# First pass of a decoder layer: the state sums of two neighbouring units done together on TensorE

## The chip, the cores and the metric

The kernel runs on one core of one Trainium2 chip. The metric is device time in microseconds of one execution, lower is better. Times given for the kernel are the median of several runs; the rows shown come from one profiled execution.

## The reference, cut to what matters

The layer takes 128 sequences of 128 tokens with 256 features and passes them through a Mamba block, a cross-attention block with a state-space convolution, and a feed-forward block with nine paths. The change lies in the Mamba block (inner width 512, 16 states):

```python
xz = einsum('bld,ed->ble', x, in_proj_w);  xc, z = split(xz, 2)
xs = silu(causal_conv(xc, conv_w) + conv_b)
dt, Bm, Cm = split(xs @ x_proj_w.T, [64, 80])
dt = softplus(dt @ dt_proj_w.T + dt_proj_b);  A = -exp(A_log)
# over the tokens, for each channel d and state n:
h[d, n] = exp(dt[d] * A[d, n]) * h[d, n] + dt[d] * Bm[n] * xs[d]
y[d] = sum_n h[d, n] * Cm[n] + D[d] * xs[d]
out = (y * silu(z)) @ out_proj_w.T
```

Then, in the same pass of the kernel, the first half of cross attention: query and key projections, scores of 4 heads, the 32 largest of each row, softmax over them, their mean over heads times the context, and the linear maps (film) that scale and shift the normed input.

## The kernel before

Everything is float32. The kernel has a set-up part and three passes. The first pass does the Mamba block and the attention part, the second the state-space convolution, the third the feed-forward block. Only the first pass is touched.

The first pass works in 32 blocks of four sequences (512 columns). A block has 64 units, `u` = 0 to 63: four chunks `c` of 128 channels by 16 states `n`, so a unit is the scan of one state of one chunk over 512 columns. Each engine has its own program with a loop over the units; they meet through semaphores that count (`need(engine, name, i, k)` waits until event `name` of block `i` has happened `k` times). What a unit does:

- ScalarE writes the decay exp(dt A) (L1044), into PSUM for an even unit and into SBUF for an odd one.
- The input term dt B x is made in two ways. For an even unit GpSimd multiplies it into the ring (L1263, event `bx`). For an odd unit ScalarE scales it in transposed form (L1031, `bxt`), and TensorE transposes it back with four transposes (`spread_bx`, L860, `bxp`), one unit ahead (`PE_AHEAD` = 1).
- VectorE runs the scan (L1175 for odd units, L1179 for even ones, event `scan`) into a slot of a ring of eight (`RING` = 8).
- GpSimd multiplies the state by C (L1250, event `hc`), four units behind (`POOL_LAG` = 4).
- TensorE adds the product to y in PSUM, a matmul with the identity (`sum_states`, L875, event `nsum`), also four units behind (`SUM_LAG` = 4). The first sum of a chunk (`n` = 0) also starts the bank with diag(D) times xs (L874). This frees the slot of the ring: the input product or scan eight units on waits for it. After the 16th sum of a chunk ScalarE copies y out (L1022) at unit `n` = 2 of the next chunk.

Between these, each engine runs "steps" at fixed units, from tables `PE_AT`, `ACT_AT`, `DVE_AT` and `POOL_AT` (step name: unit). Steps of `FRONT` prepare the next block `i + 1`, steps of `BACK` finish block `i - 1`. On TensorE the even units with steps are 2, 6, 8, 10, 14, 22, 24, 26, 30, 34, 36, 40, 42, 44, 54, 56, 58, 60 and 62. The steps that the text speaks of:

- `sc0` to `sc3` (units 22, 29, 36, 45): scores of one sequence, one bf16 matmul for the mask (L817) and four heads with 32 rows each (L824). All four use one bank: `sc2` waits until VectorE has read the bank for sequence 1 (`em`, L1147), at the end of a search in four rounds (`tka` to `tkd`, L1132 and L1136) and the exponentials on ScalarE (`sm`, L989 and L993). `qk` (unit 21) makes q and k, copied out by ScalarE (k in L984).
- `xp` (unit 24): x_proj (L745), needs ScalarE's silu (L928); `bt` (unit 26): transposes of B and C (L758), need ScalarE's copy of x_proj (L936).
- `dt0` to `dt3` (L752), read by ScalarE (L950, L952); `ds0` to `ds3` (L774 and after), the softplus sum, copied by ScalarE (L966) and multiplied by GpSimd (L1242).
- `op0` to `op3` (L785): out_proj; `tu0` to `tu3` (L767): transposes of dt x, copied by ScalarE (L942); `xc0` to `xc3` and `z0` to `z3` (L739): in_proj, with the convolution's taps on VectorE (L1099).

All steps but the scores share two PSUM banks in turn, so a step also waits until the tile before the last has been read (`take_bank`). TensorE's program is in order: a step or sum that waits holds up what is behind it.

Of the kernel before, what the change touches and what calls it, by code (L numbers as in the profile page):

```python
# [49 lines left out]
SUM_LAG = 4  # L50
# [57 lines left out]
def steps_at(table, u, which):  # L108

    return [s for s, at in table.items() if at == u and s in which]  # L110
# [35 lines left out]
def through_pe(u):  # L146

    return u % 2 == 1
# [340 lines left out]
def pass1(nc, sems, i_, arena, psum, x1_d, xa_d, xin_d, wf_d, bc_d, kr_d, sh, NB):  # L489
    with ExitStack() as ctx:  # L490
# [77 lines left out]
        def need(eng, name, i, k):  # L568

            count = i * PER[name] + k  # L570
            if not isinstance(count, int) or count > 0:
                eng.wait_ge(S[name], count)
# [12 lines left out]
        def which_steps(front, back):  # L585
            return (FRONT if front else []) + (BACK if back else [])
# [125 lines left out]
        def _(pe):  # L712
# [140 lines left out]
            def spread_bx(i, u):  # L853

                v = u // 2
                need(pe, "bxt", i, v + 1)
                j, w = before(i, u, 4)
                need(pe, "scan", j, w + 1)
                for b in range(G):
                    mm = pe.transpose(bx_ps[:, v % 2, b * L:(b + 1) * L], bxt[:, v % 2, b * P:(b + 1) * P], ident)  # L860
                mm.then_inc(S["bxp"], 1)

            def sum_states(i, par, u):
                if u < 0:
                    i, par, u = i - 1, 1 - par, C * NS + u
                need(pe, "hc", i, u + 1)
                c, n = u // NS, u % NS
                if n == 0:
                    if c == 0:
                        need(pe, "y", i - 1, C)  # L870
                    else:
                        need(pe, "y", i, c)

                    pe.matmul(y_ps, diag_d[:, c], xs[par][:, c], start=True, stop=False)  # L874
                pe.matmul(y_ps, ident, ring[:, u % RING], start=False, stop=n == NS - 1).then_inc(S["nsum"], 1)  # L875

            def iteration(i, par, front, back):
                which = ([True] if front else []) + ([False] if back else [])
                names = which_steps(front, back)
                for u in range(C * NS):  # L880
                    w = u + PE_AHEAD
                    if through_pe(w):
                        if w < C * NS:
                            spread_bx(i, w)
                        elif front:
                            spread_bx(i + 1, w - C * NS)
                    if u >= SUM_LAG or back:
                        sum_states(i, par, u - SUM_LAG)
                    for s in steps_at(PE_AT, u, names):
                        if s in FRONT:  # L890
                            step(s, i + 1, 1 - par, i - 1, which)
                        else:
                            step(s, i - 1, 1 - par, i + 1, which)
# [7 lines left out]
            for u in range(PE_AHEAD):  # L901
                if through_pe(u):
                    spread_bx(0, u)
            all_blocks(pe, iteration, NB)
            for u in range(SUM_LAG):
                sum_states(NB, 0, u - SUM_LAG)
# [1029 lines left out]
```

## Time and profile before

| | |
|---|---|
| runs, us | 7264.4, 7266.84, 7272.13; median 7266.84 |
| profiled execution, us | 7281.31 |
| its span, us | 7279.5 |
| mean granted TensorE clock | 0.947 of full |
| first pass | from about 250 us to 5100 us of the span |
| busy share of the span | TensorE 92%, VectorE 74%, GpSimd 63%, ScalarE 61% |

Times in the profile are microseconds from the start of the span unless marked ns. A line of the timeline gives start, duration, engine, source line, operation, destination and source with their shapes, and how many instructions of one kind in a row were merged (x4). In brackets stand the idle time of the engine before it and what ended it. A float32 matmul over 512 columns is two records, each with a weight load on a row of its own (PEld). Matmuls overlap, so the sum of durations is more than the time that passes. DVE is VectorE, ACT ScalarE, POOL GpSimd. The whole of a block is some 152 us; the rows below are from one block in the middle (2500 to 2650 us) where not said otherwise.

### The profile page before, as it was taken

The numbers are of one execution on the slowest core, as the hardware profiler recorded it, in microseconds if no ns is written. First come the engines' busy times: TensorE is split into PE (matmuls) and PEld (weight loads), VectorE is DVE, ScalarE is ACT, GpSimd is POOL, SyncE is SP. The second block draws the span as 40 slices with busy tenths as digits, with TensorE's granted clock in tenths as the row PEclk, the third lists the DMA queues.
The fourth block names the chain that finished last, engine by engine and source line by source line (L and its number), as shares of the span: only waits on it lengthen the run. The fifth ranks groups of instructions, "written<-read, shape, count | busy, mean of one in ns | idle before, by whom it ended". The sixth has DMA issues, their size and how long they took to land. (4 is left out here: it accounts for less than half of the span.)

```text
span 7279.5 us, 106079 instructions
## 1 busy us (share of the span) xinstructions
PE 6712.2 (92%) x24272; PEld 3702.6 (51%) x24272; DVE 5405.5 (74%) x13962; ACT 4456.3 (61%) x9788; POOL 4589.0 (63%) x3991
## 2 busy tenths in 40 slices
PE   2899999999999999999999999997789999999997
PEld 1354444544445444454445544454656666666664
DVE  5588888888888888888888888887436666666665
ACT  2778888788877888878888788885212112221111
POOL 0788888888888888888888888897011112111111
PEclk6999999999999999999999999998889999999998
DMA  1666556665666666666556655566611111111110
GB/s 42 137 142 151 140 144 156 154 146 144 143 150 153 147 144 143 152 153 149 143 135 151 158 147 144 137 151 176 208 35 33 32 32 32 32 32 32 32 32 20
DMA packets 554199, 834.94 MB, mean 115 GB/s; under 512 B 169180, under 2 KB 207389, under 8 KB 551713
## 3 DMA queue, kind: packets, MB, share of 16 engines
q1 hardware_dynamic: 552768, 820.23, 46.1%
q10 hardware_dynamic: 864, 8.65, 0.3%
q8 instruction: 174, 2.85, 0.2%
q14 instruction: 393, 3.21, 0.1%
HBM read 745.91 MB, written 74.45 MB: 113 GB/s over the span
## 5 line engine op out<-in xcount | busy, mean ns | idle before, releaser
L1250 POOL TENSOR_TENSOR arena<-arena 128x512 f32<-128x512 f32 x2048 | 2581.9, 1276 | 276.4 <-DVE arena L1175 249.2
L875 PE MATMUL psum<-arena 128*128 128x512 f32 x4096 | 2192.3, 632 | 43.7 <-POOL arena L1250 37.9
L1175 DVE TENSOR_TENSOR_SCAN arena<-arena,psum 128x512 f32<-128x512 f32 x1024 | 1237.2, 1208 | 385.4 <-ACT arena L1044 297.9
L1263 POOL TENSOR_TENSOR arena<-arena 128x512 f32<-128x512 f32 x1024 | 1331.6, 1300 | 149.8 <-PE psum L875 149.5
L1031 ACT ACTIVATE arena<-arena 128x128 f32<-128x128 f32 x4096 | 1304.8, 396 | 134.0 <-PE psum L860 133.6
L1179 DVE TENSOR_TENSOR_SCAN arena<-psum,arena 128x512 f32<-128x512 f32 x1024 | 1234.8, 1206 | 87.4 <-ACT psum L1044 26.0
L875 PEld LDWEIGHTS psum<-arena 128*128 128x128 f32 x4096 | 712.0, 199 | 599.0 <-issue 385.4
L1044 ACT ACTIVATE arena<-arena 128x508 f32<-128x508 f32 x1024 | 738.5, 721 | 57.8 <-DVE arena L1175 57.1
L1829 POOL TENSOR_SCALAR arena<-arena 128x4 f32<-128x4 f32 x160 | 37.0, 231 | 1164.9 <-DVE arena L1690 1164.9
L860 PEld LDWEIGHTS psum<-arena 128*128 128x128 f32 x4096 | 518.7, 146 | 489.2 <-issue 441.4
L1044 ACT ACTIVATE psum<-arena 128x508 f32<-128x508 f32 x1024 | 701.5, 685 | 64.8 <-DVE arena L1179 31.0
L860 PE MATMUL psum<-arena 128*128 128x128 f32 x4096 | 648.1, 283 | 27.1 <-DVE arena L1175 12.5
L1653 ACT ACTIVATE arena<-psum,arena 128x512 f32<-128x512 f32 x256 | 176.5, 690 | 621.6 <-PE psum L1560 621.6
L739 PE MATMUL psum<-arena 128*128 128x512 f32 x1024 | 479.7, 597 | 29.9 <-ACT arena L1068 27.5
L1560 PE MATMUL psum<-arena 128*128 128x512 f32 x1024 | 449.9, 597 | 1.4 <-ACT arena L1647 1.4
L1571 PE MATMUL psum<-arena 128*128 128x256 f32 x2048 | 447.2, 379 | 0.0
L1571 PEld LDWEIGHTS psum<-arena 128*128 128x128 f32 x2048 | 388.9, 190 | 66.7 <-issue 15.4
L1136 DVE MATCH_REPLACE8 arena<-arena 128x128 f32<-128x128 f32 x1536 | 407.1, 278 | 0.0
L1838 POOL TENSOR_TENSOR arena<-arena 128x1024 f32<-128x1024 f32 x32 | 75.3, 2353 | 448.1 <-DVE arena L1728 448.1
L1099 DVE SCALAR_TENSOR_TENSOR arena<-psum,arena 128x508 f32<-128x508 f32 (+2 forms) x384 | 282.6, 743 | 98.7 <-ACT arena L919 89.5
L739 PEld LDWEIGHTS psum<-arena 128*128 128x128 f32 x1024 | 195.6, 192 | 277.7 <-issue 267.6
L1132 DVE MAX8 arena<-arena 128x8 f32<-128x128 f32 x1536 | 327.8, 277 | 7.7
(218 smaller groups left out, 10103.8 us busy)
## 6 DMA issues: line engine op xcount, KB each, us to landing
arena<-bc_scratch SPq DMA_DIRECT2D x1152, 512.0 KB, 5.3
arena<-in_xT_dram SPq DMA_DIRECT2D x32, 512.0 KB
arena<-in_x_dram SPq DMA_DIRECT2D x32, 512.0 KB, 7.8
x_scratch<-arena SPq DMA_DIRECT2D x32, 512.0 KB, 5.7
xin_scratch<-arena SPq DMA_DIRECT2D x128, 128.0 KB, 2.5
arena<-kernel_scratch SPq DMA_DIRECT2D x32, 512.0 KB, 7.0
arena<-x_scratch SPq DMA_DIRECT2D x32, 512.0 KB, 3.8
out_dram<-arena SPq DMA_DIRECT2D x32, 512.0 KB
```

Of the source, the lines that this page charges most:

```text
L739: mm = pe.matmul(ps, win[:, k, e0:e0 + P], xT[:, k], start=k == 0, stop=k == DH - 1)
L860: mm = pe.transpose(bx_ps[:, v % 2, b * L:(b + 1) * L], bxt[:, v % 2, b * P:(b + 1) * P], ident)
L875: pe.matmul(y_ps, ident, ring[:, u % RING], start=False, stop=n == NS - 1).then_inc(S["nsum"], 1)
L1031: a = act.activation(bxt[:, v % 2, b * P:(b + 1) * P], uT(par, c)[:, b * P:(b + 1) * P], ACT.Identity, scale=BT[par][:, b, state(u):state( ...
L1044: act.activation(seqs(decay)[:, :, 1:L], seqs(dt[par][:, c])[:, :, 1:L], ACT.Exp, scale=negA[:, c, k:k + 1]).then_inc(S["decay"], 1)
L1136: a = dve.match_replace(left[:, h], v8[:, r, h], src[:, h], NEG)
L1175: dve.tensor_tensor_scan(s, decay_sb[:, u // 2 % 2], bx_ps[:, u // 2 % 2], 0.0, ALU.mult, ALU.add)\
L1179: dve.tensor_tensor_scan(s, decay_ps[:, u // 2 % 2], s, 0.0, ALU.mult, ALU.add)\
L1250: pool.tensor_tensor(h, h, Cb[:, u // 2 % PAIRS, u % 2], ALU.mult).then_inc(S["hc"], 1)
L1263: pool.tensor_tensor(ring[:, u % RING], uu[par][:, c], Bb[:, state(u)], ALU.mult)\
L1560: mm = pe.matmul(psum[:, m % 2], w1[:, k, m * P:(m + 1) * P], hT[:, k], start=k == 0, stop=k == DH - 1)
L1571: mm = pe.matmul(psum[:, 2 + o, bb * D:(bb + 1) * D], gT[:, m, b * L:(b + 1) * L], w2[:, m], start=m == 0, stop=m == 7)
```

## The change

In TensorE's loop over the units the state sum that lies four units behind used to be issued in every unit, ahead of the unit's steps. Now an even unit issues none, and an odd unit issues two: the one that lies five units behind (the even one) and the one that lies four behind. The transposes of `spread_bx`, which are issued in even units, so stand between the pairs. Nothing else is edited.

```diff
                         elif front:
                             spread_bx(i + 1, w - C * NS)
-                    if u >= SUM_LAG or back:
-                        sum_states(i, par, u - SUM_LAG)
+                    if u % 2:
+                        for w in (u - SUM_LAG - 1, u - SUM_LAG):
+                            if w >= 0 or back:
+                                sum_states(i, par, w)
                     for s in steps_at(PE_AT, u, names):
                         if s in FRONT:
                             step(s, i + 1, 1 - par, i - 1, which)
```

## Rows read from the trace of the kernel before

**Rows 1.** The page, part 1: busy us, share of the span, instructions.

```profile
PE 6712.2 (92%) x24272; PEld 3702.6 (51%) x24272; DVE 5405.5 (74%) x13962; ACT 4456.3 (61%) x9788; POOL 4589.0 (63%) x3991
```

**Rows 2.** Groups by line and shape, 1000 to 5000 us: busy, mean, idle before, releaser.

```profile
L1250 POOL TENSOR_TENSOR arena<-arena 128x512 f32<-128x512 f32 x1685 | 2124.7, 1276 | 223.9 <-DVE arena L1175 206.1 <-DVE arena L1179 14.3 <-DMA arena<-bc_scratch 1.9
L875 PE MATMUL psum<-arena 128*128 128x512 f32 x3366 | 1800.9, 631 | 30.0 <-POOL arena L1250 25.9
...
L875 PEld LDWEIGHTS psum<-arena 128*128 128x128 f32 x3366 | 584.7, 199 | 481.1 <-issue 314.4 <-POOL arena L1250 157.6
```

**Rows 3.** Timeline of TensorE around scores 2: start, us, engine, line, count, idle before.

```profile
2552.58 1.88 PE L875 MATMUL psum<-arena 128*128 128x512 f32 x4
...
2558.69 1.10 PE L874 MATMUL psum<-arena 128*128 128x512 f32 x2
2559.62 1.02 PE L875 MATMUL psum<-arena 128*128 128x512 f32 x2
...
2565.02 0.60 PE L817 MATMUL psum<-arena 1*128 1x512 bf16 x1 [3.32 <-DVE arena L1147]
...
2568.52 2.08 PE L875 MATMUL psum<-arena 128*128 128x512 f32 x2
```

**Rows 4.** Timeline of VectorE from scores 0 to unit 31.

```profile
2533.83 0.89 DVE L1132 MAX8 arena<-psum 128x8 f32<-128x128 f32 x4 [0.70 <-PE psum L824]
...
2550.39 1.20 DVE L1175 TENSOR_TENSOR_SCAN arena<-arena,psum 128x512 f32<-128x512 f32 x1
```

**Rows 5.** Timeline of all engines, units 22 to 26.

```profile
2530.15 0.59 ACT L984 COPY arena<-psum 128x512 f32<-128x512 f32 x1 [1.08 <-PE psum L806]
...
2531.49 0.38 PE L817 MATMUL psum<-arena 1*128 1x512 bf16 x1
...
2533.83 1.91 ACT L928 ACTIVATE arena<-arena 128x2048 f32<-128x2048 f32 x1
...
2535.91 3.60 PE L745 MATMUL psum<-arena 128*96 128x512 f32 x8
...
2541.26 0.57 ACT L936 COPY arena<-psum 96x512 f32<-96x512 f32 x1
...
2541.92 0.40 PE L758 MATMUL psum<-arena 32*128 32x32 f32 x4 [0.26 <-issue]
```

**Rows 6.** Timeline of TensorE at unit 30, the transposes for unit 31.

```profile
2548.68 0.66 PE L860 MATMUL psum<-arena 128*128 128x128 f32 x4
```

**Rows 7.** Timeline of TensorE one block earlier, scores 0 and scores 2.

```profile
2378.49 0.39 PE L817 MATMUL psum<-arena 1*128 1x512 bf16 x1
...
2414.59 0.60 PE L817 MATMUL psum<-arena 1*128 1x512 bf16 x1 [2.71 <-DVE arena L1147]
```

**Rows 8.** Timeline of ScalarE in that block, unit 34.

```profile
2408.20 0.59 ACT L1022 COPY arena<-psum 128x512 f32<-128x512 f32 x1 [4.04 <-PE psum L875]
```

**Rows 9.** Timeline of GpSimd after scores 2.

```profile
2573.24 1.71 POOL L1263 TENSOR_TENSOR arena<-arena 128x512 f32<-128x512 f32 x1 [4.05 <-PE psum L875]
...
2586.26 1.09 POOL L1242 TENSOR_TENSOR arena<-arena 128x512 f32<-128x512 f32 x1 [3.63 <-ACT arena L966]
```

**Rows 10.** Timeline of TensorE, units 43 to 50, the gaps.

```profile
2582.00 1.12 PE L774 MATMUL psum<-arena 128*128 128x512 f32 x2 [0.28 <-ACT arena L1009]
...
2595.83 1.13 PE L875 MATMUL psum<-arena 128*128 128x512 f32 x2 [0.21 <-POOL arena L1250]
...
2598.30 1.93 PE L875 MATMUL psum<-arena 128*128 128x512 f32 x3 [0.47 <-POOL arena L1250]
```

**Rows 11.** Timeline of all engines at unit 60.

```profile
2622.35 0.56 ACT L942 COPY arena<-psum 128x512 f32<-128x512 f32 x1
...
2623.55 0.60 PE L767 MATMUL psum<-arena 128*128 128x128 f32 x4
```

**Rows 12.** Timeline of all engines at unit 8.

```profile
2644.22 2.31 DVE L1099 SCALAR_TENSOR_TENSOR arena<-psum,arena 128x508 f32<-128x508 f32 x3 [0.46 <-ACT arena L919]
...
2647.07 1.24 PE L785 MATMUL psum<-arena 128*128 128x256 f32 x5
```

## The prediction

> **What bounds the kernel now.** I read the page first, then the groups of instructions, and last the timelines of single engines through one block. The page's busy shares [rows 1] put TensorE (92%) ahead of VectorE (74%), GpSimd (63%) and ScalarE (61%), but they average over three passes. The change touches the first pass alone, which repeats one block of 64 units (four sequences) 32 times. The reader should see in the timelines that the period of a block has two parts with different limits.
>
> *Part one, scores 0 to scores 2.* VectorE waits 0.70 us for the first scores and starts its top-k search at 2533.83; from there to scores 2 its timeline shows no idle row, with the scan of unit 31 at 2550.39 [rows 4]. TensorE is ahead: before scores 2 it stands idle for 3.32 us until VectorE's masked exponentials (L1147) are done [rows 3]. A wait like this one stands there in each of the 30 steady blocks.
>
> *Part two, scores 2 to scores 0 of the next block.* TensorE goes from group to group with small gaps only, of which the largest are 0.28, 0.21 and 0.47 us [rows 10]. Right after the wait it runs at 1.2 GHz, half its clock: a state sum (two records) takes 2.08 us there against 1.02 before it [rows 3].
>
> Blocks come in two kinds. From scores 0 to scores 2 this one takes 2565.02 - 2531.49 = 33.53 us [rows 3, 5], the one before it 2414.59 - 2378.49 = 36.10 us [rows 7]. There TensorE fell to half clock once more, just after scores 1; ScalarE then stood idle 4.04 us for state sum 31, which it needs to read y [rows 8], and the exponentials came late through ScalarE, not through VectorE. Of the 30 waits before scores 2, 14 are of the first kind (about 3.3 us) and 16 of the second (about 2.7).
>
> **The change, part by part.** *Work removed or added: none.* Matmuls, weight loads, semaphore waits and DMAs stay the same in number, and the queues of SP, GpSimd, ScalarE and VectorE are not edited. In an even unit without a step the order on TensorE stays what it was: transposes, even sum, odd sum. So the edit does one thing: in the 19 even units that have steps, the steps come ahead of the even sum.
>
> *Is a pair of sums cheaper than two apart?* Two sums in a row take 1.88 us, one takes 1.02, so the second adds 0.86 [rows 3]; that is the spacing of matmuls, with the loads (199 ns each [rows 2]) under running matmuls. I take 0. The bound on the other side is one load saved per pair, 1024 x 0.199 = 204 us, but the diff removes no load, and each matmul has its own (3366 and 3366 [rows 2]).
> The Trainium skill ("TensorE: Matmul & The Clock Gate", Part 2, Step-by-step) says that weights usually stay across many matmuls, so that one load serves several. By it the pair, both with the identity, could gain up to that bound; this case's trace disagrees with its one load per matmul.
>
> *Scores 0 (unit 22) ahead of sum 18.* They start at 2531.49; k's copy ends at 2530.15 + 0.59 = 2530.74 [rows 5]. Without a sum (0.86) before them they could start at 2530.63 and so at about 2530.85: 0.64 earlier, with 0.2 us of idle TensorE. VectorE waits for just this [rows 4], so its dense stretch begins 0.64 earlier: a gain.
>
> *x_proj (24) ahead of sum 20, B/C transposes (26) ahead of sum 22.* Silu ends at 2533.83 + 1.91 = 2535.74 and x_proj starts at 2535.91; 0.86 earlier it would wait about 0.6. ScalarE's copy of x_proj ends at 2541.26 + 0.57 = 2541.83 and the transposes already wait 0.26 for it [rows 5]; moved ahead they still start at 2541.92, and the sum that covered the wait comes behind. These delays overlap: TensorE is late by about 0.75 us from unit 28 on (0.86 less the gap of some 0.1). Queued behind are the transposes for unit 31, now 2548.68 with an end near 2549.3 [rows 6]. They would end at 2550.05, and VectorE's scan would want them at 2550.39 - 0.64 = 2549.75: 0.3 of the 0.64 is lost, and sum 31, late too, eats another 0.2 through ScalarE. Scores 2 then come 0.15 us earlier in a block of the first kind (bounds -0.64 and +0.3), and 0.75 later in the second, where their chain starts from sum 31 (bounds 0 and +0.86). Mean (14 x -0.15 + 16 x 0.75)/30 = **+0.33 us**.
>
> *Scores 2 (36) ahead of sum 32*, the largest piece. Sum 32 opens a chunk, so it is L874 and L875 together, two matmuls of 0.86 = 1.72 us of work [rows 3]. Today they fill time in which TensorE waits anyway; afterwards they stand behind scores 2 and belong to part two. There the gaps of 0.28 + 0.21 + 0.47 = 0.96 us are set by ScalarE and GpSimd and can close. That leaves 0.76; if GpSimd's products stay last at 2598.30 [rows 10] it is 0; if they move along, 1.72. GpSimd's product for unit 40 waits for sum 32 and comes at about 2572; this lies under its waits of 4.05 and 3.63 us [rows 9], and would cost 2 to 3 us without them. I take **+0.4 us**, between closed gaps and GpSimd as the last.
>
> *The other even steps.* out_proj (8), now at 2647.07, could go at 2646.21, but its bank is free when VectorE's taps end, 2644.22 + 2.31 = 2646.53: 0.35 idle [rows 12]. tu3 (60), now at 2623.55, could go at 2622.69, but its bank is read until 2622.35 + 0.56 = 2622.91: 0.25 [rows 11]. For the others I find the operands ready 0.86 us earlier, or a wait that something later covers. Their sums come one to four us later; at cost 0, since GpSimd makes three state products and one input product of about 1.3 us each (5 us) between the product that a sum reads and the one that waits for the sum. Bounds 0 and 0.6; I take the middle, **+0.3 us**.
>
> **Sum.** 0.33 + 0.4 + 0.3 = 1.03 us per block; on 30 blocks +31 us. The profiled execution took 7281.31 us for a span of 7279.5; the runs' median, 7266.84, is 14.5 lower, and the terms are the same for both. Predicted: 7266.84 + 31 = **7298 us** (+0.4%), own range 7282 to 7325.
>
> **Rivals.**
> *Absorbed.* Part two swallows the moved sum (term 0), and VectorE's earlier start pays for x_proj's wait. For it: the 3.32 us of idle TensorE in part one; against it: the second kind of block, where TensorE is last already. 7255 to 7281, within 0.2%.
> *Half clock in every block.* Transposes, 32-row scores and 64-row dt matmuls now follow each other at units 22, 30 and 36, and idle time is added at 24 and 26. If TensorE falls to half clock after scores 1 in all blocks, the 14 of the first kind take 36.10 - 33.53 = 2.57 us more: +36, 7334 us. For it: 16 blocks do so now, with the same program [rows 7]; against it: the other 14.
> The Trainium skill (same page, Part 4) says that a transpose does not count as a busy TensorE as a matmul does. By it, taking the sums from between transposes and scores brings that same loss; no row here tells the kinds of work apart.
> *Faster.* Scores 0 start 0.64 earlier and VectorE's whole dense stretch moves with them, the rest being absorbed: -0.64 x 30 = -19, 7248 us. It decides if the transposes for unit 31 are late by less than 2550.39 - 0.64 - 2549.3 = 0.45 us. Were the second low-clock stretch to go as well, 16 x 2.57 = 41 us more, 7207.
> *Pairing saves loads.* Up to 204 us; nearly nil, as above.
>
> **How the numbers follow.** Forecast 0.50, absorbed 0.22, half clock everywhere 0.14, faster by VectorE's chain 0.12, loads 0.02. About 0.2% (14.5 us) is what a measurement of this kernel can tell from no change. Slower 0.50 + 0.14 = 0.64, same 0.22, faster 0.12 + 0.02 = 0.14. The range leaves out most of the fast cases and the far end of the slow ones: 7255 to 7335.
>
> **What the profile after would show.** Scores 0 right behind their transposes; a VectorE idle of about 0.3 us for TensorE at scan 31; idle TensorE ahead of x_proj, and more of it ahead of the B/C transposes; L874 behind scores 2, at half clock; GpSimd's first long idle after scores 2 longer and earlier; the gaps of 0.28 to 0.47 us smaller or gone; the block some 1 us longer. The prediction fails if the number of low-clock stretches changes, or if part two has more room than its gaps show.

## The result and the profile after

The changed kernel takes **7414.38 us** (median of 4 runs, 7404.76 to 7417.88) against 7265.62 us (7260.88 to 7272.13) for the kernel before on the same chip: ratio **1.0202**, 95% interval 1.0184 to 1.0220. That is 149 us more, where 31 were forecast. The profiled execution took 7404.76 us (span 7403.0), 123.5 more than that of before. The two differences do not agree because the profiled execution of before was a long one (7281.31) and that of after its shortest; what is read from traces below is to be held against 123.5.

The page of the changed kernel, to hold against [rows 1] (busy us, share of the span, instructions):

```profile
PE 6763.8 (91%) x24272; PEld 3735.4 (50%) x24272; DVE 5420.0 (73%) x13962; ACT 4458.1 (60%) x9788; POOL 4619.8 (62%) x3991
```

No instruction went or came. TensorE is busy 51.6 us longer with the same matmuls, so part of them ran slower; the other 72 us are time in which it is not busy. Groups by line and shape, 1000 to 5000 us, against [rows 2]:

```profile
L875 PE MATMUL psum<-arena 128*128 128x512 f32 x3276 | 1674.3, 632 | 14.4 <-POOL arena L1252 5.9
...
L875 PEld LDWEIGHTS psum<-arena 128*128 128x128 f32 x3276 | 611.3, 199 | 713.5 <-issue 557.9 <-POOL arena L1252 148.8
```

A load still stands before each matmul (3276 and 3276) and the mean is 632 ns against 631: the pair of sums saved nothing. The waits of GpSimd's input product for the sums, same window, before and after (us in total, times, longest):

```profile
POOL arena L1263 <- PE psum L875: 123.6, 44, 4.1
```

```profile
POOL arena L1265 <- PE psum L875: 379.4, 211, 6.9
...
PE psum L817 <- DVE arena L1149: 89.7, 26, 3.5
```

They tripled. The wait before scores 2 is still there (26 times, 3.45 us on average), in every block of the window.

The timeline of TensorE after the change; the first stretch answers to [rows 5], that at 1449 is the turn of the loop, and that from 2164.17 answers to [rows 3]:

```profile
1344.76 0.49 PE L860 MATMUL psum<-arena 128*128 128x128 f32 x3
1345.54 0.37 PE L817 MATMUL psum<-arena 1*128 1x512 bf16 x1 [0.29 <-ACT arena L986]
1345.76 2.00 PE L824 MATMUL psum<-arena 32*128 32x128 f32 x8
1347.69 1.98 PE L875 MATMUL psum<-arena 128*128 128x512 f32 x4
1349.51 0.60 PE L860 MATMUL psum<-arena 128*128 128x128 f32 x4
1350.35 3.68 PE L745 MATMUL psum<-arena 128*96 128x512 f32 x8 [0.24 <-ACT arena L930]
...
1356.48 0.40 PE L758 MATMUL psum<-arena 32*128 32x32 f32 x4 [0.29 <-issue]
...
1449.47 0.65 PE L860 MATMUL psum<-arena 128*128 128x128 f32 x4 [1.88 <-issue]
...
2164.17 0.60 PE L817 MATMUL psum<-arena 1*128 1x512 bf16 x1 [3.45 <-DVE arena L1149]
2164.57 3.17 PE L824 MATMUL psum<-arena 32*128 32x128 f32 x8
2167.67 2.08 PE L874 MATMUL psum<-arena 128*128 128x512 f32 x2
...
2176.04 2.37 PE L875 MATMUL psum<-arena 128*128 128x512 f32 x4 [0.51 <-POOL arena L1252]
```

The reader should see the order as forecast: scores 0 right behind the transposes with 0.29 us of idle time, the pair of sums (L875 x4) behind them, an idle row ahead of x_proj (0.24 us), and L874 behind scores 2 at half clock (2.08 us). GpSimd's first long wait after scores 2, [rows 9], began earlier, 0.5 us behind the start of scores 2 instead of 4.2, and grew from 4.05 to 6.91 us:

```profile
1388.76 3.21 POOL L1265 TENSOR_TENSOR arena<-arena 128x512 f32<-128x512 f32 x1 [6.91 <-PE psum L875]
```

**A block in four segments.** Because the scores cut each block in four, I measured the starts of the four mask matmuls (L817) in 26 steady blocks of each trace. Here are two blocks in which TensorE's clock fell only about scores 2, first one of before, then one of after. Columns:  window, its length, busy us of each engine (instructions), granted clock, share and GB/s of the DMA engines. The engines stand in the order TensorE, its weight loads, VectorE, ScalarE, GpSimd.

```profile
1770.35:1785.38 15.03, 14.60 (x50) 6.78 (x50) 13.56 (x62) 14.94 (x29) 12.32 (x10) 1.00 0.57 138
1785.38:1803.88 18.50, 14.94 (x53) 7.00 (x53) 18.05 (x66) 17.09 (x44) 16.85 (x14) 0.96 0.65 140
1803.88:1828.65 24.77, 24.28 (x66) 11.80 (x66) 22.35 (x69) 24.50 (x52) 15.59 (x14) 0.82 0.35 90
1828.65:1920.10 91.45, 90.03 (x325) 48.81 (x325) 73.80 (x138) 68.34 (x165) 87.00 (x78) 1.00 0.75 169
```

```profile
2130.05:2146.41 16.36, 15.68 (x51) 7.35 (x52) 15.38 (x63) 16.27 (x33) 13.48 (x12) 1.00 0.56 129
2146.41:2164.17 17.76, 13.17 (x48) 6.51 (x48) 16.92 (x65) 15.52 (x40) 16.18 (x14) 0.92 0.60 146
2164.17:2190.47 26.30, 25.50 (x70) 12.39 (x70) 23.21 (x70) 26.03 (x56) 17.91 (x14) 0.86 0.32 88
2190.47:2282.02 91.55, 89.55 (x323) 48.54 (x323) 72.69 (x137) 66.97 (x161) 85.64 (x76) 1.00 0.72 169
```

These two blocks differ by 151.97 - 149.75 = 2.22 us, and the third segment (scores 2 to scores 3) holds 1.53 of it. The means over the 26 blocks differ by more. "Low" is the time at 1.2 GHz, worked out from the granted clock g of a segment of length l as 2 (1 - g) l:

| us | 0 to 1 | 1 to 2 | 2 to 3 | 3 to next 0 | block | low 0 to 1 | low 1 to 2 | low 2 to 3 |
|---|---|---|---|---|---|---|---|---|
| before | 15.19 | 19.69 | 25.14 | 92.17 | 152.18 | 0.39 | 4.36 | 8.90 |
| after | 17.10 | 20.09 | 26.45 | 92.59 | 156.22 | 2.49 | 6.79 | 8.31 |

The block is 4.04 us longer: 121 us on 30 blocks, 125 on 31, which is all of the 123.5. Low time between scores 1 and 2 costs nothing where it falls into the wait before scores 2, as it does in the two blocks shown. Blocks in which the clock did not fall ahead of that wait are 14 of 30 in before and 7 of 30 in after. The trace of before is of an execution 15 us longer than the kernel's median. Traces of two kernels below that take as long as before and change nothing there (sums 2 to 14 late, sum 58 late) have 2.79 and 3.22 us of low time between scores 1 and 2, so some 1 us of before's 4.36 is likely to belong to this execution.

### The profile page after: what moved, and what is told of

The parts are those of the page before. It is cut to its first block and busy times, and to the rows that moved or that the text cites. A ratio compares the mean times of both kernels' runs of the same rounds, so it can differ in the third digit from the quotient of the medians.

```text
span 7403.0 us, 106079 instructions
## 1 busy us (share of the span) xinstructions
PE 6763.8 (91%) x24272; PEld 3735.4 (50%) x24272; DVE 5420.0 (73%) x13962; ACT 4458.1 (60%) x9788; POOL 4619.8 (62%) x3991
## 5 line engine op out<-in xcount | busy, mean ns | idle before, releaser
L875 PE MATMUL psum<-arena 128*128 128x512 f32 x4096 | 2093.8, 631 | 30.9 <-POOL arena L1252 19.7
L875 PEld LDWEIGHTS psum<-arena 128*128 128x128 f32 x4096 | 761.8, 199 | 904.7 <-issue 684.2
L860 PEld LDWEIGHTS psum<-arena 128*128 128x128 f32 x4096 | 513.6, 146 | 501.8 <-issue 438.7
L1655 ACT ACTIVATE arena<-psum,arena 128x512 f32<-128x512 f32 x256 | 176.3, 689 | 621.8 <-PE psum L1562 621.8
L739 PE MATMUL psum<-arena 128*128 128x512 f32 x1024 | 479.9, 597 | 30.6 <-ACT arena L1070 28.2
L1562 PE MATMUL psum<-arena 128*128 128x512 f32 x1024 | 449.9, 597 | 1.4 <-ACT arena L1649 1.4
L1573 PEld LDWEIGHTS psum<-arena 128*128 128x128 f32 x2048 | 389.0, 190 | 66.7 <-issue 15.4
L1661 ACT ACTIVATE arena<-psum,arena 128x512 f32<-128x512 f32 x64 | 40.6, 685 | 459.3 <-PE psum L1581 459.2
```

Source lines behind the costliest of these rows:

```text
L739: mm = pe.matmul(ps, win[:, k, e0:e0 + P], xT[:, k], start=k == 0, stop=k == DH - 1)
L1562: mm = pe.matmul(psum[:, m % 2], w1[:, k, m * P:(m + 1) * P], hT[:, k], start=k == 0, stop=k == DH - 1)
L1573: mm = pe.matmul(psum[:, 2 + o, bb * D:(bb + 1) * D], gT[:, m, b * L:(b + 1) * L], w2[:, m], start=m == 0, stop=m == 7)
```

## The experiments

Two theories stood at the start. **Order**: the sums of some even units are late where TensorE's queue has no room, above all sum 32 behind scores 2. **Clock**: with the sums taken from between narrow work, TensorE falls to 1.2 GHz more often. Both needed the change taken apart by unit. One edit to the kernel before does this; `LATE` lists the even units whose sum goes behind the steps, all 32 being the changed kernel and none the kernel before:

```diff
+LATE = (22, 24, 26)
...
-                    if u >= SUM_LAG or back:
-                        sum_states(i, par, u - SUM_LAG)
+                    late = LATE if u % 2 else ()
+                    for w in ([u - SUM_LAG - 1] if u - 1 in late else []) + ([u - SUM_LAG] if u not in LATE else []):
+                        if w >= 0 or back:
+                            sum_states(i, par, w)
```

In these kernels TensorE's lines stand one higher than in the kernel before and most others three higher. Each was timed in the same rounds as the kernel before; the us behind a ratio are the difference of the two medians.

### One piece at a time

```diff
+LATE = (22, 24, 26)
```


> Only the even sums of units 22, 24 and 26 go behind their steps, all others stay ahead. Theory W (each moved sum costs through waits on TensorE where it was cover): part one of the block, scores 0 to scores 2, grows as it did in the changed kernel, less the sum that only changed sides: +0.9 to +1.5 us a block, +28 to +46 us in all. Theory G (GpSimd runs short of ring slots because sums come late in bunches, mostly behind long steps late and early in the block): under +15 us, since these steps are short. Theory C (the loss is time at half clock and follows from where the blocks fall): no fixed share, but the half-clock time per block, 13.8 us before and 17.6 after, rises by over 2 us wherever the time rises.

Measured: 7340.07 us, 1.0090 (1.0071 to 1.0109), +62 us.

```diff
+LATE = (36,)
```


> Only sum 32, with the chunk's first matmul, goes behind unit 36's steps. Theory W: 1.72 us of work moves behind the wait for scores 2 and part two has under 1 us of gaps: +0.8 to +1.6 us a block, +25 to +50 us. Theory G: the product for unit 40 comes 6 us late, but is covered by GpSimd's later waits: 0 to +15 us. Theory C: no change of half-clock time, so 0 to +10.

Measured: 7343.86 us, 1.0092 (1.0074 to 1.0110), +66 us.

```diff
+LATE = (54, 56, 58, 60, 62)
```


> Only the even sums of units 54 to 62 go behind their steps (xa, film0 to film3, tu3). Theory W: only tu3's bank wait, +0.25 us a block, +8 us. Theory G: GpSimd has no idle time here in the kernel before, and in the changed one it waits for sums (0.17 to 0.60 us each) and TensorE's gap at the block's boundary is 2.04 us against 0.65: +1 to +1.5 us a block, +30 to +45 us.

Measured: 7316.38 us, 1.0062 (1.0042 to 1.0082), +38 us.

```diff
+LATE = (2, 6, 8, 10, 14)
```


> Only the even sums of units 2, 6, 8, 10 and 14 go behind their steps. Theory W: out_proj's bank wait, +0.35 us a block, +11 us. Theory G: GpSimd waits 0.97 and 0.25 us for sums here in the changed kernel: up to +1 us a block, +30 us. If all parts are additive, the four runs and the one for units 30 to 44 together make +149 us.

Measured: 7280.72 us, 1.0012 (0.9999 to 1.0025), +3 us, not clear of noise.

```diff
+LATE = (30, 34, 40, 42, 44)
```


> Only the even sums of units 30, 34, 40, 42 and 44 go behind their steps (dt1, dt2, at1, ds0, ds2). The parts run so far gave +62 (22 to 26), +66 (36), +38 (54 to 62) and +3 us (2 to 14), 169 against 149 for all together. Additive theory: -20 us here. Theory W: dt1, dt2, ds0 and at1 find their operands ready, so 0 to +10 us, and the parts overlap rather than add.

Measured: 7332.87 us, 1.0090 (1.0074 to 1.0106), +66 us.

The parts make 62 + 66 + 38 + 3 + 66 = 235 us; the whole is 149. So no piece carries the change, and they share costs. The segments tell where each pays:

| us | 0 to 1 | 1 to 2 | 2 to 3 | 3 to next 0 | block | low 0 to 1 | low 1 to 2 | low 2 to 3 |
|---|---|---|---|---|---|---|---|---|
| 22, 24, 26 | 17.44 | 19.64 | 25.44 | 91.70 | 154.22 | 3.54 | 4.37 | 7.32 |
| 36 | 15.51 | 19.75 | 27.27 | 91.84 | 154.37 | 1.18 | 4.67 | 8.06 |
| 30 to 44 | 15.78 | 19.86 | 26.24 | 91.61 | 153.49 | 1.84 | 4.32 | 6.44 |
| 54 to 62 | 15.30 | 19.43 | 25.13 | 93.31 | 153.17 | 0.66 | 3.54 | 8.41 |
| 2 to 14 | 15.14 | 19.15 | 24.97 | 92.23 | 151.50 | 0.26 | 2.79 | 9.03 |

*Sum 32 alone* costs 2.13 us in the third segment. The timeline of TensorE in that run:

```profile
2447.07 0.60 PE L818 MATMUL psum<-arena 1*128 1x512 bf16 x1 [3.45 <-DVE arena L1150]
2447.47 3.17 PE L825 MATMUL psum<-arena 32*128 32x128 f32 x8
2450.57 2.08 PE L875 MATMUL psum<-arena 128*128 128x512 f32 x2
...
2458.63 1.12 PE L876 MATMUL psum<-arena 128*128 128x512 f32 x2 [1.23 <-POOL arena L1253]
...
2462.33 1.12 PE L876 MATMUL psum<-arena 128*128 128x512 f32 x2 [0.84 <-POOL arena L1253]
```

and that of GpSimd:

```profile
2454.04 1.27 POOL L1266 TENSOR_TENSOR arena<-arena 128x512 f32<-128x512 f32 x1 [6.50 <-PE psum L876]
2455.27 4.54 POOL L1253 TENSOR_TENSOR arena<-arena 128x512 f32<-128x512 f32 x2
```

The diag matmul runs at half clock behind scores 2. GpSimd's input product for unit 40 waits 6.50 us for the sum that frees its slot, and the state products queued behind it come late; TensorE then waits for those (1.23 and 0.84 us). The prediction had this wait as hidden under GpSimd's other waits. It is not: GpSimd's queue carries it back to TensorE.

*The sums of units 30 to 44 alone* cost 1.10 us there, in waits for ScalarE:

```profile
2446.51 1.12 PE L777 MATMUL psum<-arena 128*128 128x512 f32 x2 [1.21 <-ACT arena L966]
...
2454.62 1.13 PE L775 MATMUL psum<-arena 128*128 128x512 f32 x2 [0.88 <-ACT arena L969]
```

The softplus sums of units 42 and 44 go ahead of their state sum. The first finds its operand not written (the logarithm, L966 here), the second its bank not read (the copy, L969 here). The prediction had these as ready. One wait more grows in the next segment, in every block: the transposes of unit 53 (L831, `at3`) wait 0.88 us for ScalarE in this run and in the changed kernel, 0.38 us in before.

*The sums of units 54 to 62 alone* pay in the last segment, +1.14 us. The prediction had forecast a wait at tu3 and missed one at the step that averages the heads (xa0). Its bank is the one of `tu0`, so it waits until ScalarE has copied that tile (L945 here):

```profile
1254.47 2.17 PE L841 MATMUL psum<-arena 128*128 128x128 f32 x16 [0.48 <-ACT arena L945]
```

Two splits of this group:

```diff
+LATE = (62,)
```


> Only sum 58 goes behind film3, the last step before the loop of two blocks turns back. Theory L (the pair at the very end of the loop leaves nothing to cover the turn): the visible idle of TensorE at the turn is 1.4 us or more in 13 turns, against 5 visible ones before, +0.7 us a block, +15 to +25 us. Theory of the banks (xa and tu3): nothing here, within 7 us of before.

Measured: 7263.19 us, 1.0005 (0.9993 to 1.0016), +3 us, not clear of noise.

```diff
+LATE = (54, 56, 58, 60)
```


> The even sums of units 54 to 60 go behind their steps, 58 stays. Theory of the banks: xa waits 0.48 us for the copy of tu0, tu3 0.25 us for that of tu2: +0.9 us a block, +20 to +35 us, scores 3 to the next scores 0 0.9 us longer in blocks without a turn. Theory L: the turn's visible idle stays as before.

Measured: 7294.26 us, 1.0047 (1.0031 to 1.0063), +34 us. Unit 62 costs nothing. The four others carry 34 of the 38 us (last segment 92.84 us; with 62 as well 93.31, alone 91.97). The other wait of the group stands at the turn of the loop (two blocks are one pass of it, so 13 turns in the 26 blocks). TensorE's idle time ahead of the first transposes there, over the 13 turns, is 0.73 us on average in before, 1.43 with the whole group, 0.53 with unit 62 alone and 0.33 with the four alone: it takes both.

### Which of units 22, 24 and 26

```diff
+LATE = (22,)
```


> Only sum 18 goes behind scores 0. Theory W (the gain is real, x_proj and the B/C transposes lose it again): scores 0 some 0.6 us earlier, VectorE's dense stretch with it, -10 to -20 us. Theory C (a run of transposes and 32-row scores without a sum between brings half clock right behind scores 0): the half-clock time between scores 0 and scores 1 rises from 0.4 us a block to over 2, and the time by 20 to 50 us.

Measured: 7346.66 us, 1.0108 (1.0092 to 1.0124), +79 us.

```diff
+LATE = (24, 26)
```


> Only sums 20 and 22 go behind x_proj and behind the B/C transposes; sum 18 stays between the transposes and scores 0. Sum 18 alone gave +79 us, with 3.8 us of half clock a block between scores 0 and scores 1. Theory K (the half clock comes from transposes, 64-row and 32-row matmuls with no full matmul between them): half clock there under 1 us a block, time +10 to +30 us. Theory W (waits of TensorE ahead of x_proj and the transposes): +28 to +60 us.

Measured: 7311.07 us, 1.0064 (1.0051 to 1.0077), +46 us.

Sum 18 alone, an edit that takes nothing from anyone and lets scores 0 start earlier, costs as much as any other piece. With sums 20 and 22 late as well it was +62, and these two alone cost +46: the intervals of +79 and +62 overlap, so all that can be said is that the two add nothing to it. Of the theories, C held for sum 18 (and the cost was above its range), and for sums 20 and 22 the time was in W's range, though low time between scores 0 and 1 was 1.05 us a block. The timeline of TensorE with sum 18 alone late:

```profile
1476.47 1.12 PE L807 MATMUL psum<-arena 64*128 64x512 f32 x2
1477.52 0.66 PE L861 MATMUL psum<-arena 128*128 128x128 f32 x4
1478.47 0.37 PE L818 MATMUL psum<-arena 1*128 1x512 bf16 x1 [0.29 <-ACT arena L987]
1478.68 2.31 PE L825 MATMUL psum<-arena 32*128 32x128 f32 x8
1480.92 3.78 PE L876 MATMUL psum<-arena 128*128 128x512 f32 x4
1484.49 1.06 PE L861 MATMUL psum<-arena 128*128 128x128 f32 x4
1485.35 1.77 PE L876 MATMUL psum<-arena 128*128 128x512 f32 x2
1486.95 3.60 PE L746 MATMUL psum<-arena 128*96 128x512 f32 x8
```

Four records of the sums take 3.78 us where they take 1.88 at full clock, four transposes 1.06 instead of 0.60. The granted clock between scores 0 and the x_proj is 0.63:

```profile
1478.47:1484.40 5.93, 5.76 (x13) 2.85 (x14) 5.13 (x19) 5.90 (x8) 4.24 (x5) 0.63 0.68 151
```

In the lines shown ahead of the drop TensorE was not idle, but for 0.29 us. What differs from before is what it did: a product of 64 rows, four transposes, the mask of one row and scores of 32 rows, with no full matmul (128 rows, 512 columns) in between; in before a sum stood between the transposes and the mask. Low time between scores 0 and 1 went from 0.39 to 3.81 us a block, and the segment from 15.19 to 17.42. The order by itself cost nothing, as far as this trace can show it. None of its 26 blocks is free of low clock ahead of scores 2, but its shortest segments, each from a block where the clock did not fall in it or fell only in the wait and behind it, add up to 15.58 + 17.76 + 25.44 + 90.90 = 149.68 us, against 149.75 for before. With sums 20 and 22 late as well, such a block takes 150.50, some 0.8 us more (24 us over the kernel), which is x_proj's and the B/C transposes' delay.

### All but one piece

```diff
+LATE = tuple(u for u in range(0, 64, 2) if u != 36)
```


> The changed kernel, but sum 32 with the chunk's first matmul stays ahead of unit 36's steps. Additive: 149 - 66 = +83 us against before. If the part of unit 36 counts only when it is alone (others already late): over +120 us.

Measured: 7405.58 us, 1.0181 (1.0164 to 1.0197), +138 us. Sum 32 is worth only 11 us when the others are late too, which is within the noise of the two ratios, against 66 alone. At full clock ahead of scores 2 such a block takes 151.94 us, the changed kernel's 151.97. Its segment from scores 2 to scores 3, and the three waits of TensorE in it:

```profile
1692.73:1719.02 26.29, 23.74 (x66) 11.50 (x66) 23.10 (x70) 26.02 (x56) 17.52 (x14) 0.87 0.33 89
```

```profile
1706.41 1.13 PE L777 MATMUL psum<-arena 128*128 128x512 f32 x2 [1.25 <-ACT arena L966]
...
1710.37 1.13 PE L775 MATMUL psum<-arena 128*128 128x512 f32 x2 [0.26 <-ACT arena L1012]
...
1714.53 1.12 PE L775 MATMUL psum<-arena 128*128 128x512 f32 x2 [0.88 <-ACT arena L969]
```

The segment is as long as the changed kernel's (26.30), without the 1.72 us of sum 32 in it. TensorE is idle for ScalarE instead, at the softplus sums. In the changed kernel's block from 2164.17 on these waits are gone and sum 32 stands in their place; TensorE is busy 25.50 us there, ScalarE 26.03 as here. So the two costs lie side by side, and the longer one counts.

```diff
+LATE = tuple(u for u in range(0, 64, 2) if u != 22)
```


> The changed kernel (+149 us), but sum 18 stays ahead of scores 0. Theory K: half clock between scores 0 and scores 1 falls from 2.5 us a block to under 1, and the time to +70 to +115 us. Theory W: keeping sum 18 there only takes away the earlier start of scores 0: +149 us or more.

Measured: 7399.87 us, 1.0186 (1.0173 to 1.0199), +134 us: between the two theories, and within the noise of the changed kernel's +149.

```diff
+LATE = tuple(u for u in range(0, 64, 2) if u not in (22, 30))
```


> As all_but_22, and sum 26 stays between the transposes behind scores 1 and dt1. Theory K: the half clock between scores 1 and scores 2 falls too (5.7 us a block in the changed kernel), to 3.5 or less, and the time is 15 to 40 us below all_but_22. Theory W: the same as all_but_22 within 10 us.

Measured: 7376.37 us, 1.0153 (1.0140 to 1.0166), +111 us. Sum 18 put back halves the low time between scores 0 and 1 (2.49 to 1.31 us a block) and gives some 15 us back at most; sum 26 back as well, some 23 more, which is clear of noise and what theory K asked for (low time between scores 1 and 2 from 6.65 to 3.94). What one sum costs depends on what else has been taken from around it.

### The clock by itself

If a full matmul between narrow ones (of few rows) keeps the clock, then one put there should make the kernel before faster. Before scores 1 its order is sum, dt0 (64 rows), scores 1 (32 rows), transposes. One number moves dt0 a unit up, ahead of the sum:

```diff
-             ... dt0=29, sc1=29, ...
+             ... dt0=28, sc1=29, ...
```


> The kernel before, but dt0 goes from unit 29 to unit 28, so that sum 25, a full matmul, stands between dt0 (64 rows) and scores 1 (32 rows). Theory K: fewer blocks fall to half clock behind scores 1 (3.4 us a block before), down to 1.5 us or less: -15 to -35 us. Theory W: nothing is waited for here: 0 to -5 us.

Measured: **7241.24 us**, 0.9973 (0.9962 to 0.9984), 24 us faster than the kernel before and the best of all. A block at full clock is not shorter (149.83 us against 149.75), so this gain is the clock's alone: low time between scores 1 and 2 fell from 4.36 to 1.26 us a block, and what of it lies ahead of the wait from 3.28 to 0.39. The segment went from 19.69 to 18.34 us. (1.35 us a block would be 40 us; before's trace is of a long execution, and the medians say 24.) The same edit in the changed kernel:

```diff
+LATE = all 32 even units
-             ... dt0=29, sc1=29, ...
+             ... dt0=28, sc1=29, ...
```


> The changed kernel (+149 us) with dt0 at unit 28, so that two sums stand between dt0 and scores 1. Theory K: half clock between scores 1 and scores 2 falls from 5.7 us a block to under 3, and the time by 25 to 50 us against the changed kernel: +100 to +125 us. If the waits of the changed order rule: +140 us or more.

Measured: 7359.81 us, 1.0133 (1.0117 to 1.0148), +103 us: with 1.0202 for the changed kernel, it takes back 0.69% or about 50 us, as theory K said. Low time from scores 1 to 2: 6.79 to 3.88, in a profiled execution that was 27 us longer than this kernel's median; that from scores 0 to 1 rose from 2.49 to 3.28.

The same idea at scores 0: of q and k, k comes last, and its second product (L807, 64 rows) stands right ahead of the transposes. I made k before q, so that q's full products stand there, and had ScalarE copy them in that order. First on the kernel with sum 18 late, then on the best one:

```diff
-TILES = dict(... qk=["q", "k"], ...
+TILES = dict(... qk=["k", "q"], ...
```


> late_22 (sum 18 behind scores 0, +79 us), but unit 21 makes k (its second matmul has 64 rows) before q (128 rows), and ScalarE copies them in that order. The two full matmuls of q then stand between the 64-row one and the transposes. Theory K: the 3.8 us a block of half clock between scores 0 and scores 1 fall to under 1.5, and the time to +10 to +45 us. If order inside the unit does not matter to the clock: +70 to +90 us as before.

Measured: 7327.69 us, 1.0097 (1.0077 to 1.0118), +68 us. Low time from scores 0 to 1 fell from 3.81 to 2.36 us: in the direction of the theory, but far less than it asked for. The time is outside K's range, and against late_22's 1.0108 (1.0092 to 1.0124) it is not clear of noise.

> The order of the kernel before, dt0 at unit 28, and k made before q. dt0 alone gave -24 us; k before q took about 15 us off late_22. Theory K: it takes the last 0.5 us a block of half clock behind scores 0: -24 to -32 us. If k before q only helps where sum 18 is late: -24 us.

Measured: 7254.39 us, 0.9992 (0.9983 to 1.0001). By the ratios it takes some 14 us of dt0_28's 20 away, and both theories miss; the two intervals just touch. The traces explain part of it: a block at full clock ahead of scores 2 takes 150.03 us against 149.83, 6 us over the kernel, and the clock fell behind scores 0 or 1 in 9 of 26 blocks against 7 (low time between scores 1 and 2 is 1.34 us a block against 1.26, between scores 0 and 1 the same 0.53). What is left stays open.

Last, low time behind scores 2, the largest piece of it. Scores 2 one unit later, behind sum 33:

```diff
-             ... dt3=36, sc2=36, ...
+             ... dt3=36, sc2=37, ...
```


> The kernel before, but scores 2 move from unit 36 to unit 37, so that sum 33 too is ahead of the wait for VectorE. The reverse of the changed kernel's step at unit 36. Theory W: 0.86 us of work goes from behind the 3.3 us wait to inside it, and 0.4 us less of it runs at half clock: -0.9 to -1.2 us a block, -25 to -40 us. Theory of slack (part two has room for such work, as the prediction took it): -10 us or less.

Measured: 7267.91 us, 0.9998 (0.9988 to 1.0009). So theory W is wrong and the theory of slack right. Low time from scores 2 to 3 fell from 8.90 to 4.33 us a block, and the segment stayed: 25.14 and 25.00. In the block shown it is 24.76 us with a granted clock of 0.93, against 24.77 with 0.82 above:

```profile
1960.69:1985.45 24.76, 21.51 (x63) 10.05 (x64) 23.13 (x69) 24.50 (x52) 15.26 (x14) 0.93 0.38 90
```

and its TensorE stands idle instead:

```profile
1968.80 0.63 PE L832 MATMUL psum<-arena 128*128 128x128 f32 x4 [0.64 <-ACT arena L1006]
...
1971.61 0.66 PE L861 MATMUL psum<-arena 128*128 128x128 f32 x4 [1.33 <-DVE arena L1178]
...
1977.66 1.13 PE L775 MATMUL psum<-arena 128*128 128x512 f32 x2 [1.10 <-ACT arena L1012]
```

TensorE is busy 21.51 us there instead of 24.28, and ScalarE 24.50 us in both. So in this segment TensorE and ScalarE were level in the kernel before: less work and less low time for TensorE are worth nothing, since ScalarE stays full, and while work moved into it cost time (+2.13 us for sum 32 alone).

Both edits together:

```diff
-             ... dt0=29, sc1=29, ... dt3=36, sc2=36, ...
+             ... dt0=28, sc1=29, ... dt3=36, sc2=37, ...
```


> No sum moved; dt0 at unit 28 (alone -24 us) and scores 2 at unit 37 (alone 0). If half clock behind scores 1 is what dt0 saved and scores 2 at 37 saves half clock that nothing waits for: -24 us, +-8. If both shorten the part they stand in: -40 us or better.

Measured: 7242.57 us, 0.9977 (0.9966 to 0.9987), -17 us: nothing on top of dt0_28, as the first theory said.

A ring of more slots, which might have freed GpSimd from the late sums, was not tried.

## Why the prediction was right or wrong

The direction was right, the size was not: 7298 forecast, 7414 measured, outside the range of 7255 to 7335. Per block, 1.03 us were forecast and 4.04 found in the traces (which differ by 123.5 us and not by the medians' 149; how the other 25 us divide is not known):

| | forecast | found |
|---|---|---|
| part one, scores 0 to 2, without clock | +0.33 | +0.15 |
| segment scores 2 to 3 (forecast: scores 2 ahead of sum 32) | +0.4 | +1.53 |
| segment scores 3 to next 0 (forecast: the other even steps) | +0.3 | +0.89 |
| the clock | 0 (a rival) | +1.47 |

The first three are from blocks without low clock ahead of scores 2, as the two shown: scores 0 to 2 takes 34.15 us instead of 33.53, less the 0.47 by which scores 0 start earlier behind their transposes (1.45 us before, 0.98 after); then 24.77 and 26.30; then the last segment, +0.42 in the mean, plus that 0.47. The clock is the rest, 4.04 - 2.57 = 1.47. The other kind of block gives much the same: where the clock fell once ahead of scores 2, behind scores 1, scores 0 to 2 takes 37.30 us (two blocks of after) against 36.09, and scores 2 to 3 takes 26.29 against 25.45, +2.05 together against +2.15 for the first kind. Its part one, +1.21 less the 0.47, is the 0.75 that the prediction had for it.

- *Pairing saves nothing:* right. No load went. The Trainium skill ("TensorE: Matmul & The Clock Gate", Part 2, Step-by-step) says that weights typically stay across many matmuls; this kernel's rows have one load for each, in a pair too.
- *Scores 0 earlier:* right in kind. They start earlier by 0.47 us and not by 0.64, with an idle time of 0.29 instead of 0.2.
- *x_proj and B/C transposes wait:* right in kind (0.24 us against 0.6, and 0.29), and part one as a whole came out small, as forecast. VectorE then stands 0.30 to 0.34 us at scan 31, forecast 0.3.
- *Part two, scores 2 ahead of sum 32:* **the step that failed**, with the clock below. The prediction put 0.4 us on the segment behind scores 2: 1.72 us of sums come in, gaps of 0.96 us close, GpSimd's wait stays hidden, and the softplus sums of units 42 and 44 find their operands ready, at cost 0. The segment grew by 1.53 us. Of the gaps only the first (0.28) lies between scores 2 and 3, where TensorE was busy 24.28 of 24.77 us and ScalarE 24.50. Run alone, sum 32 costs 2.13 us there, through GpSimd's queue. But the same 1.53 us come without it: with sum 32 back in its place the segment is 26.29 us, by TensorE's waits of 1.25 and 0.88 us for ScalarE at the softplus sums. So the term has no size of its own, and that is the deeper fault: terms that pass through one queue were priced one by one and summed (the five pieces make 235 us alone, 149 together).
- *The other even steps:* a term of 0.3 with an upper bound of 0.6; the last segment holds 0.89. The search for operands that are not ready missed xa0's wait (0.48 us with units 54 to 62 alone, 0.29 in the changed kernel) and the longer one at unit 53 (0.38 to 0.88 us; this gap is in before's blocks too, larger than the 0.28 that the prediction lists). It had no term for the turn of the loop. In blocks without a turn the segment grew by 0.09 us, in blocks with one by 0.76, and TensorE's idle time at the turn is 1.72 us on average in the 13 turns, against 0.73. Why it became longer was not settled.
- *Half clock in every block:* a rival with a chance of 0.14, and in kind what came on top of the waits; the forecast's own sum had the clock at 0. It was priced at 36 us on top of 31. Found: low time from scores 0 to scores 2 rose from 4.75 to 9.28 us a block, +1.69 us in length there and -0.22 behind scores 2, so some 44 us of the 123.5. It was placed after scores 1; half of the rise came after scores 0 (0.39 to 2.49 us; 3 blocks of 26 in before, 16 in after), where the prediction showed no row of it. The prediction cited the Trainium skill on it (same page, Part 4: a transpose does not count as busy as a matmul does). late_22 and dt0_28 do not contradict it: a single state sum between transposes, 64-row and 32-row work, taken away or put in, changed the clock. No run tells the transposes from the narrow matmuls, and dt0_28_kq and the small effect of late_22_kq show that the order of such work alone does not foretell the clock.
- *Absorbed* and *faster by VectorE's chain:* wrong. In the block from 2130.05 on, VectorE's earlier start of 0.47 us was eaten by the 0.30 us at scan 31 and by 0.17 us before the masked exponentials: there ScalarE, which waited 2.17 us for sum 31 instead of 1.35, was last. The prediction had 0.3 and 0.2 for these two.

What stays open: why k ahead of q takes back most of the gain of dt0_28, why the turn of the loop costs more, and how the waits divide between order and clock in a single block, since a late clock and a late sum stretch each other.

## What to carry to other kernels

Before giving an edit a discount for gaps, take the busy share of every engine in just that segment; where two are near one (24.28 and 24.50 of 24.77 us here), take the upper bound. For each step that is moved ahead, look up who writes its operand and who reads its bank, and when. Costs of moving several instructions in one queue don't add up; cost the whole order at once or try the pieces. Before taking wide matmuls from between narrow ones and transposes, look at the granted clock after such stretches; putting one there (dt0_28) gained 24 us here at no cost.

## What the runs showed of the hardware

- TensorE's clock fell to 1.2 GHz with no idle time of over 0.3 us in the twelve us ahead of scores 0, after a stretch of 64-row products, transposes and 32-row products (late_22, granted clock 0.63 in the 5.9 us from scores 0 on). Moving one sum of 0.86 us out of that stretch cost 79 us over the kernel; moving a 64-row product to the other side of a sum gained 24 us.
- The same program has more or fewer such stretches from run to run: runs of the kernel before lie between 7238 and 7293 us, and blocks with and without one (149.75 and 152.99 us) stand side by side in one trace.
- A lower clock is not always paid for: 4.6 us a block less of it behind scores 2, where ScalarE is busy 24.50 of 24.77 us, changed the time by nothing (sc2_37), 3.1 us less behind scores 1 gained 24 us (dt0_28).
- At the turn of TensorE's loop the queue stands idle: 0.73 us on average over 13 turns in before (up to 2.35), 1.72 in after, put down to "issue" or to ScalarE's L1031. The kernel's order of work changed it (0.33 to 1.72 us over the runs); no run shows what it is.
